# Marks on PE, short roots, sequence 0 first, and POOL's 128x512 products on DVE

## The reference

```python
kv = ctx @ W_k.T + b_k                                   # layer 0 attention
sim = (LN(x) @ kv) @ kv.T * 512**-0.5                    # p is LN(x), 512 x 512
x = x + softmax(LN(sim) * gamma + beta)
h = LN(x)                                                # layer 0 ffn
dense = rms(gelu(rms(h) @ w_gate) * (rms(h) @ w_up) @ w_down)
moe = rms(sum over the top 2 of 8 experts of aff * expert(rms(h)))
x = x + rms(dense + moe)
q, k = rms(LN(x)), rms(ctx); rope; 16 heads on 4 kv heads, causal; @ w_out.T   # layer 1 attention
x = x + attention
x = x + (silu(LN(x) @ w_gate.T) * (LN(x) @ w_up.T)) @ w_down.T                # layer 1 ffn
```

## Time and profile before

| | us |
|---|---|
| runs | 1896.76, 1894.06, 1890.92 (median 1894.06) |
| profiled execution | 1889.51 |
| its span | 1887.8 |
| PE busy | 1700.5 |
| DVE busy | 1145.1 |
| ACT busy | 797.8 |
| POOL busy | 269.6 |

### The profile page before, as it was taken

The page is one execution under the profiler, slowest core; times in us unless marked ns, Lnnn a source line. Parts: engine busy times, 40 slices in busy tenths (PEclk is TensorE's granted clock), DMA queues, the critical chain, the costliest instruction groups (busy, mean ns, idle before and its releaser), DMA issues. The chain is left out here.

```text
span 1887.8 us, 27233 instructions
## 1 busy us (share of the span) xinstructions
PE 1700.5 (90%) x9396; PEld 1349.7 (71%) x9396; DVE 1145.1 (61%) x2506; ACT 797.8 (42%) x1789; POOL 269.6 (14%) x270
## 2 busy tenths in 40 slices
PE   3688988599988999787999999978999999999998
PEld 3576876488887987665767667766776678678887
DVE  6798777255665745984566766689646563553222
ACT  4465553143665753322555555433245452431111
POOL 1224126523121203220000000222100000000000
PEclk8699988799999999998999999988989999999999
DMA  3325567389789887779335316988873445236562
GB/s 108 107 101 179 167 195 270 121 317 346 252 271 328 279 306 295 241 274 303 94 118 158 106 46 202 383 297 317 270 235 105 125 123 204 77 125 209 186 219 97
DMA packets 127063, 384.93 MB, mean 204 GB/s; under 512 B 15680, under 2 KB 30416, under 8 KB 121168
## 3 DMA queue, kind: packets, MB, share of 16 engines
q1 hardware_dynamic: 119088, 360.61, 56.6%
q0 software_dynamic: 7840, 22.59, 3.5%
HBM read 278.78 MB, written 104.37 MB: 203 GB/s over the span
## 5 line engine op out<-in xcount | busy, mean ns | idle before, releaser
L1185 PE MATMUL ps<-xT,gu 128*128 128x512 f32 (+1 forms) x1392 | 535.0, 384 | 78.5 <-DVE act L1662 31.7
L1187 PE MATMUL ps<-xT,gu 128*128 128x512 f32 (+1 forms) x1392 | 514.5, 370 | 4.0 <-issue 4.0
L1186 PE MATMUL ps<-xT,gu 128*128 128x512 f32 (+1 forms) x1392 | 514.3, 369 | 4.1 <-issue 4.1
L1185 PEld LDWEIGHTS ps<-xT,gu 128*128 128x128 f32 x1392 | 271.3, 195 | 131.8 <-issue 39.2
L1187 PEld LDWEIGHTS ps<-xT,gu 128*128 128x128 f32 x1392 | 270.0, 194 | 49.0 <-issue 5.6
L1186 PEld LDWEIGHTS ps<-xT,gu 128*128 128x128 f32 x1392 | 270.9, 195 | 40.9 <-issue 4.8
L1185 PE MATMUL ps<-wd,hid 128*128 128x512 f32 x604 | 248.9, 412 | 28.3 <-DVE acc L1697 13.9
L1186 PE MATMUL ps<-wd,hid 128*128 128x512 f32 x604 | 239.3, 396 | 0.0
L1187 PE MATMUL ps<-wd,hid 128*128 128x512 f32 x604 | 239.0, 396 | 0.0
L1390 ACT ACTIVATE hid<-act 128x512 fp32r<-128x512 f32 (+1 forms) x174 | 100.0, 575 | 281.0 <-DVE act L1662 278.2
L1662 DVE TENSOR_TENSOR act<-act,ps 128x512 f32<-128x512 f32 (+1 forms) x174 | 106.8, 614 | 157.7 <-PE ps L1187 150.8
(11 more groups left out here) (277 smaller groups left out, 2282.5 us busy)
## 6 DMA issues: line engine op xcount, KB each, us to landing
gu<-w_dram SPq DMA_DIRECT2D x160, 512.0 KB
raw<-in_ffn_w SPq DMA_DIRECT2D x94, 768.0 KB
wd<-w_dram SPq DMA_DIRECT2D x80, 512.0 KB, 5.6
w_dram<-gu SPq DMA_DIRECT2D x32, 1024.0 KB
w_dram<-wd SPq DMA_DIRECT2D x32, 512.0 KB
QT<-q_dram SPq DMA_DIRECT2D x48, 256.0 KB, 4.9
y_dram<-x SPq DMA_DIRECT2D x23, 512.0 KB
wcs<-tab_dram SPq DMA_DIRECT2D x16, 512.0 KB, 5.9
```

Of the source, the lines that this page charges most:

```text
L1185: mm(out_ap, ah, bh, start=start, stop=False)
L1186: mm(out_ap, ah, bl, start=False, stop=False)
L1187: return mm(out_ap, al, bh, start=False, stop=stop)
```

## The change

1. The scatter, its zeroing and the reload are gone. For each token tile `t`, DVE makes one-hot marks by comparing `lanes` with the slot's lane and tile (`hot`), and PE multiplies them into PSUM bank 5 (`spot`): the sum over 32 products is the list of token numbers by lane and tile. DVE copies it to `row_of` (`rowno`).
2. `inverse_root` has two steps instead of three, the second of higher order, with the factor -0.5 folded into the input (`BETA`); `ROOT = 3`. The factor in `simstats` is folded away.
3. `held_behind` adds rules for the planner alone: `rn2`, `ctx 1`, `stats1 1` and the splits of weight tiles 0 and 1 are placed only after given steps of sequence 0.
4. The five kinds of 128x512 products and sums of POOL are DVE instructions: `gam`, `xh`, `xy` (was part of `xt`), the last of `parts`, `qsum`. The planner's costs follow.

```diff
-    ROOT = 4
+    ROOT = 3
-        return ticks + [[("scatter", n)] for n in range(NT // 2)] + [[("tokload",)]]
+        return ticks + [[item] for t in range(NT) for item in (("hot", t), ("spot", t))] + [[("rowno",)]]
...
+    def held_behind(item):
+        if item[0] == "w" and item[1] < 2:
+            return [("stats2", 0, TB + ROOT - 1)]
+        return {("rn2",): [("simstats", 0, TB + ROOT - 1)], ("ctx", 1): [("rown", 1, 0, 1)], ("stats1", 1, 0): [("rowt", 1, 0, 1)]}.get(item, [])
...
-                on = [o for o in builds_on(item) if o not in inside and min(o[1:], default=0) >= 0]
+                on = [o for o in builds_on(item) + held_behind(item) if o not in inside and min(o[1:], default=0) >= 0]
...
-            "rown": [("ACT", 0.71)], "pkv": [("PE", 2.73), ("ACT", 0.5), ("DVE", 0.6)], "sim": [("PE", 0.68)], "scale": [("ACT", 0.67)], "gam": [("POOL", 1.25)],
...
+            "rown": [("ACT", 0.71)], "pkv": [("PE", 2.73), ("ACT", 0.5), ("DVE", 0.6)], "sim": [("PE", 0.68)], "scale": [("ACT", 0.67)], "gam": [("DVE", 0.6)],
...
-                    for t in (2 * n, 2 * n + 1):
-                        for k in range(2):
-                            nc.gpsimd.indirect_dma_start(row_dram, bass.IndirectOffsetOnAxis(ap=place[:, k, t:t + 1], axis=0), tokens[:, t:t + 1], None).then_inc(rows_placed, 16)
...
+                elif kind == "spot":
+                    t = a[0]
+                    pe.wait_ge(hot_ready, t + 1)
+                    for k in range(2):
+                        last = mm(ps[:, 5, 0:NB * RB], lane_hot[:, t % 2, k, :], tile_hot[:, t % 2, k, :], start=(t, k) == (0, 0), stop=(t, k) == (NT - 1, 1))
+                    last.then_inc(spotted, 1)
...
                 if step == 0:
                     link(V_.tensor_scalar(z.bitcast(I32), v.bitcast(I32), 1, None, ALU.logical_shift_right))
-                    link(V_.tensor_scalar(y.bitcast(I32), z.bitcast(I32), -1.0, 1597463007.0, ALU.mult, ALU.add))
-                    link(V_.tensor_scalar(v, v, -0.5, None, ALU.mult), True)
+                    link(V_.tensor_scalar(y.bitcast(I32), z.bitcast(I32), -1.0, 1597463007.0 + 1073741824.0, ALU.mult, ALU.add), True)
+                    return
+                link(tt(out=z, in0=y, in1=y, op=ALU.mult))
+                link(tt(out=z, in0=z, in1=v, op=ALU.mult))
+                if step == 1:
+                    link(stt(out=y, in0=z, scalar=3.0, in1=y, op0=ALU.add, op1=ALU.mult), True)
                 else:
-                    link(tt(out=z, in0=y, in1=y, op=ALU.mult))
-                    link(tt(out=z, in0=z, in1=v, op=ALU.mult))
-                    link(stt(out=dst if step == ROOT - 1 else y, in0=z, scalar=1.5, in1=y, op0=ALU.add, op1=ALU.mult), True)
+                    link(stt(out=z, in0=z, scalar=40.0 / 3.0, in1=z, op0=ALU.add, op1=ALU.mult))
+                    link(stt(out=dst, in0=z, scalar=80.0, in1=y, op0=ALU.add, op1=ALU.mult), True)
...
+                elif kind == "hot":
+                    t = a[0]
+                    settled()
+                    if t == 0:
+                        dve.wait_ge(consts_ready, 7)
+                    if t > 1:
+                        dve.wait_ge(spotted, t - 1)
+                    for k in range(2):
+                        V_.tensor_scalar(lane_hot[:, t % 2, k, :], lanes[:, :], lane_of[:, k, t:t + 1], None, ALU.is_equal)
+                        last = V_.tensor_scalar(tile_hot[:, t % 2, k, :], lanes[:, 0:NB * RB], tile_of[:, k, t:t + 1], tokens[:, t:t + 1], ALU.is_equal, ALU.mult)
+                    last.then_inc(hot_ready, 1)
...
-                    stt(out=yb[:, i, :], in0=ya[:, i, :], scalar=rr[:, 1, i:i + 1], in1=postB[:, 1, :], op0=ALU.mult, op1=ALU.mult).then_inc(parted, 1)
+                    link(stt(out=yb[:, i, :], in0=ya[:, i, :], scalar=rr[:, 1, i:i + 1], in1=postB[:, 1, :], op0=ALU.mult, op1=ALU.mult), True)
+                    settled()
+                    tt(out=dn[:, i, :], in0=dn[:, i, :], in1=yb[:, i, :], op=ALU.add).then_inc(summed, 1)
```

More of the change, by code:

```diff
@@ L272, in steps @@
-            "before": [("DVE", 1.1)], "blocks": [("DVE", 1.2)], "places": [("DVE", 1.1)], "slots": [("DVE", 1.0)], "scatter": [("POOL", 5.1)], "xs": [("POOL", 2.55)],
+            "rown": [("ACT", 0.71)], "pkv": [("PE", 2.73), ("ACT", 0.5), ("DVE", 0.6)], "sim": [("PE", 0.68)], "scale": [("ACT", 0.67)], "gam": [("DVE", 0.6)],
+            "bet": [("DVE", 0.75)], "aexp": [("ACT", 0.72)], "resid": [("DVE", 0.85)], "xh": [("DVE", 0.6)], "logit": [("PE", 0.95), ("DVE", 0.1)],
+            "xy": [("DVE", 0.6)], "xt": [("ACT", 0.53), ("DVE", 0.6)], "top2": [("DVE", 1.4)], "weights": [("ACT", 0.33), ("DVE", 1.2)], "ranks": [("PE", 0.36), ("DVE", 0.4)],
@@ L273, in steps @@
+            "before": [("DVE", 1.1)], "blocks": [("DVE", 1.2)], "places": [("DVE", 1.1)], "slots": [("DVE", 1.0)], "hot": [("DVE", 0.65)], "spot": [("PE", 0.42)], "rowno": [("DVE", 0.15)], "xs": [("POOL", 2.55)],
             "xgt": [("PE", 0.36), ("ACT", 0.48), ("DVE", 0.6)], "kprep": [("POOL", 4.2 if a and a[0] == 0 else 5.0 if a and a[0] > B else 4.4)], "wo": [("ACT", 0.95), ("DVE", 1.15)], "ksq": [("ACT", 1.0)],
             "kscale": [("POOL", 4.2)], "kturn": [("PE", 0.36), ("ACT", 0.5), ("DVE", 0.6)], "qtab": [("POOL", 3.4 if a and a[0] == 0 else 2.6 if a and a[0] <= TB else 1.7)], "fetch": [("POOL", 2.6)],
-            "comb": [("DVE", 1.25), ("ACT", 1.3)], "parts": [("DVE", 1.35), ("POOL", 1.3), ("ACT", 0.65)], "final": [("DVE", 2.3)], "qrow": [("ACT", 0.71), ("DVE", 1.3)],
@@ L276, in steps @@
-            "qsum": [("POOL", 1.3)], "qt": [("PE", 0.36), ("ACT", 0.48), ("DVE", 0.6)], "inv": [("DVE", 0.4)], "values": [("PE", 0.47)], "norm": [("PE", 0.22), ("ACT", 0.3), ("DVE", 0.25)],
+            "comb": [("DVE", 1.25), ("ACT", 1.3)], "parts": [("DVE", 2.1), ("ACT", 0.65)], "final": [("DVE", 2.3)], "qrow": [("ACT", 0.71), ("DVE", 1.3)],
+            "qsum": [("DVE", 0.6)], "qt": [("PE", 0.36), ("ACT", 0.48), ("DVE", 0.6)], "inv": [("DVE", 0.4)], "values": [("PE", 0.47)], "norm": [("PE", 0.22), ("ACT", 0.3), ("DVE", 0.25)],
@@ L277, in steps @@
             "split": [("ACT", 0.53), ("DVE", 0.6)], "project": [("PE", 2.85), ("DVE", 0.6)], "rown4": [("ACT", 0.71)], "rowt4": [("PE", 0.36), ("ACT", 0.48), ("DVE", 0.6)],
-            "rn2": [("DVE", 1.5), ("PE", 2.0), ("ACT", 0.5)], "zero": [("POOL", 0.75)]}.get(kind, [])
+            "rn2": [("DVE", 1.5), ("PE", 2.0), ("ACT", 0.5)]}.get(kind, [])
     def builds_on(item):
@@ L1627, in row_scales @@
                     settled()
-                    if factor is not None:
-                        link(V_.tensor_scalar(rs_[:, c], rs_[:, c], factor, None, ALU.mult))
                     stt(out=nm_[:, c], in0=mv[kind][:, c, 0], scalar=-1.0, in1=rs_[:, c], op0=ALU.mult, op1=ALU.mult).then_inc(done, 1)
```

144 lines of the change are left out of this document (67 added, 77 removed).

## The result

The changed kernel takes 1868.5 us in the median (1864.1 to 1874.2, 4 runs) against 1895.4 for the kernel before (1890.9 to 1899.9, 4 runs): ratio 0.986, interval 0.982 to 0.990. The profiled execution has a span of 1863.0 where before had 1887.8: 24.8 us less, where 31 were forecast. The forecast was 1858, with 1848 to 1868 as its own range; the median lies at the upper end of that range.

A forecast was written before the change was run, and what follows sets the result against it. PE, busy 90%, was taken as the bound, losing time idle or at half clock. Terms -24 +7 -4 +2 -10 -2 = -31 from 1889.5 gave 1858 us; own range 1848 to 1868, full range 1836 to 1880.

The forecast's parts named there:

- main term: Near 336 to 362 us: removing the scatter ends the stop of all queues and gives back 24 us, bounds 18 to 28.
- Rival 3: The stop at 336 us is not the scatter's, so the 24 us stay lost: 1882 us, chance 0.06.
- Marks: Sixteen mark steps replacing the scatter add 7 us on PE and 12 us on DVE, with PE waiting under 5 us.
- Rival 4: Marks and PE run in lock step, each mark holding PE 3 us: 1914 us, chance 0.05.
- Head: Sequence 0 first: first gate matmul near 73 us instead of 85, some PE work moved behind it, net 4 us booked.
- Products: 80 POOL products on DVE add 48 us, reduced delays give back 50; DVE busy stays within 20 us of 1145.
- I book +2: From 85 to 316 us, DVE's load changes by +4 us on 192 busy; PE's time was booked 2 us longer.
- rival 2: DVE becomes the bound of the first 12 tiles, +12 us for PE and 3 of half clock: 1873 us, chance 0.16.
- both middles and the queries: Stretches 700:900 and 1200:1400 booked at -10 us, the shorter chain to the first queries at -2.
- I book half of the 20: DVE's load falls 10 us in each middle stretch; half of that total was booked as PE time, -10 us.
- PE idle under 25 in each: Sign for the middle stretches: PE idle under 25 us in each, where it had been 32 and 30.
- under 20: Sign of being wrong: the first expert tile comes less than 20 us earlier.

The follow-up runs named there:

- a_scatter: The changed kernel with the scatter put back in place of the marks: 1882.5 us, ratio 0.9933 to the kernel before.
- b_marks: The kernel before with marks on PE and no scatter, nothing else: 1884.1 us against 1868.7, ratio 1.0094.
- a_free: The changed kernel without the planner's rule that sequence 0 goes first: 1865.8 us, ratio 0.9846 to the kernel before.
- a_poolfirst: The changed kernel with the first stages' products (gam, xh, xy) back on POOL: 1868.1 us, ratio 0.9865 to the kernel before.
- b_prod: The kernel before with all five kinds of 128x512 products and sums on DVE instead of POOL: 1852.9 us, ratio 0.9916.
- a_poolmid: The changed kernel with the last sum of parts and qsum back on POOL: 1873.2 us, ratio 0.989 to the kernel before.
- h_half: The kernel before with 16 scatters instead of 32, second choices left out: 1868.3 us against 1870.3, ratio 0.9985.
- a_paced: The changed kernel with the scatter put back and POOL waiting for landings after each four scatters: 1890.1 us, ratio 0.9958 to the kernel before.
- a_scatter_2: The changed kernel with the scatter put back, run once more on another chip: 1885.1 us, ratio 0.9931 to the kernel before.

## Why the prediction came out as it did

- **Direction and main term: right; total: 24.8 of 31.** Tiles 20 to 32 gave 25.2 where the scatter's removal was booked at 24. The stop goes with the scatter on chips of that kind: put back, it comes back (a_scatter). Rival 3, by which the stop is not the scatter's, falls for those chips. The evidence of the earlier trace rows, though, was read too strongly. No loads ran since SP had none to issue: its next load waits for DVE's weight piece, DVE for ACT, and ACT was stopped. SP's waits in the kernel before, 316 to 368 (us, times, longest), and its DMA queues, 320 to 336:

```profile
SPq L847 <- DVE wd L1677: 52.8, 4, 37.8
...
q1 hardware_dynamic: 818, 4.44, 80.1%
q0 software_dynamic: 430, 0.01, 2.1%
```

  So hardware packets took 80% of the DMA engines' time beside the software ones as long as there were loads. The Trainium skill (DMA: Bandwidth & Descriptors, SWDGE vs HWDGE vs iDMA) says that the two feed different internal queues, which a DMA engine serves in turn; the trace agrees with it as far as loads go. What stopped first was the engines' own flow, not the hardware queue. The prediction's "six of the first 15 slices" with a low clock are five; nothing hangs on it.
- **What the prediction could not see:** that the stop depends on the chip, or on a state of it. One trace holds one chip, and nothing in it says so. The forecast of 31 us was one of 24 that some chips have, and 7 of everything else; on chip C, where the 24 are not to be had, the whole change came to some 2, not to be told from none. That the trace was from a chip with the stop, and the result too, was luck.
- **Marks: right.** 7 to 8 us of PE (7 booked), 13.1 us of DVE (16 steps of 0.82; 12 booked), 1.2 us of waiting (under 5). Rival 4 falls. Yet added to the kernel before they cost 15 to 18 in all (b_marks); the part beyond PE's 7 was not taken apart.
- **Head: size right, cause half right.** First gate matmul at 74.4 (near 73 forecast), net 4.5 at tile 4 (4 booked); the fit of the 4.5 is partly luck, as the same pair of orders on chip C gives 7.8. The first gate matmul needs both parts: 79.5 without the rule (a_free), 81.2 without the first products (a_poolfirst). The net gain was booked to the rule alone, and that was wrong: without it tile 0 is as early (a_free, 87.0), without the first products it is not (a_poolfirst, 95.7).
- **Products: load right, effect mis-sized.** DVE 1141.0, within 20 of 1145; delays beside POOL gone (749 ns at most, from 1783). By the Trainium skill (SBUF — State Buffer, Who interferes with whom) a DVE instruction with two SBUF inputs contends with a GpSimd one that reads SBUF; `bet` and the second product of `parts` have two, and the trace agrees. Alone the products bring 16, where 3 to 8 were expected (b_prod), and the gain stands in tiles 4 to 20, where the prediction booked no gain.
- **First tiles: a step that failed.** "I book +2" for 85 to 316, with +7 for the marks: 9 for tiles 4 to 20. It was 13, and 15 on chip C. The term behind the 2 is DVE's load, counted as +4; from tile 4 to tile 20 DVE's busy time rose by 25 (157.7 to 182.5), 8 of which stood in the head before. PE's waits for DVE in the first 12 tiles are 17 us, not over 40. The windows of tiles 4 to 12, first of before, then of the changed kernel, show where 6 of them went:

```profile
128.30:237.60 109.30, 98.12 (x464) 80.90 (x462) 88.47 (x204) 59.85 (x104) 32.73 (x24) 0.95 0.48 154
```

```profile
123.80:239.40 115.60, 100.57 (x472) 82.08 (x471) 103.23 (x265) 67.72 (x116) 0.00 (x0) 0.88 0.52 173
```

  DVE has 15 us more in it, PE 4 more idle, and the clock is lower. a_free is 5 earlier at tile 12, so a part of rival 2 was real: with the rule sequences 1 to 3 stand closer together. At tile 78 the two are level, so it costs nothing at the end.
- **Middle: the largest miss.** 12 booked for both middles and the queries; tiles 78 to 142 gave 4.8. The step that failed is "I book half of the 20": DVE's busy time from tile 78 to 142 fell by 15 us (573.5 to 558.6), and the stretch by a third of that. In that balance 7 of each 10 us come from the roots, and the runs agree: alone, the roots shorten this stretch by 4.3, the products by 1.4. The first middle now has 24 us idle of 216, the second still 37 of 230, so one of the named signs failed (PE idle under 25 in each):

```profile
PE ps L1153 <- DVE qb L1936: 10.1, 4, 4.5
PE ps L1293 <- DMA QT<-q_dram: 7.0, 1, 7.0
PE ps L1147 <- DVE x L1668: 6.4, 3, 4.8
PE ps L1147 <- DVE gu L1648: 5.2, 1, 5.2
```

  These are PE's waits at 1170 to 1400 in the changed kernel: the sum in `qb` that DVE took over from POOL is now the longest. The likely reading, not tested, is that the chain became shorter but PE's order moved forward with it, so that PE waits for its end as before. With that sum back on POOL (a_poolmid) these rows are gone, and PE waits 14.7 us for `act` there instead. The other sign that failed: the first expert tile came 16.8 us earlier, and under 20 the prediction had called itself wrong. Its own terms up to there give 19 (-24 +7 -4 +2), so that bound did not follow from its sum; the rest is the first tiles' extra 4, less what the first two terms gave more.

What stays open is what stops the engines. PE and ACT start again at one instant, PE for 24 matmuls and ACT for one instruction, before the next gap; for PE's gaps no wait is to be seen. The rival of b_marks, instruction supply, is neither shown nor excluded: in the three traces with the gaps there are one or no packets of the instruction queues while they last, and h_half has one in 336:361 as well. Nor does any run show why some chips have the stop and two have not.

## What to carry to other kernels

Before a gain is booked from one trace, have the kernel before timed on more than one chip: here 25 of 1895 us exist on some chips only, and the change that removes them was worth 0.986 on one of these and 0.999 on one of the others. Parts that each gain alone (-16, -9, -4 on chip A) gave -1 to -2 (on chip C) together with one that costs 15 to 18, so the sum of parts measured alone (-11 to -14) is not the whole. And where a fixed order of PE was planned anew, time won early is mostly waited for later: judge at tiles where both kernels have done the same work, near the end, not by the head.

## What was not expected of the hardware

- The stop beside 32 scatters of 128 four-byte elements: 25.5 us between two chips. The same program took 1895 to 1898 us in three measurements and 1869 and 1870 in two.
- With a pause until landing after each four scatters (a landing then takes 3.1 us in the median, against 6.4 in a_scatter), no such gaps were seen through 20 scatters (a_paced), where without pauses they began by the eighteenth (a_scatter_2).
- After a DVE compare of 128x128 the next instruction starts 0.20 us later, after one of 128x46 with two operations 0.21 (changed kernel, 297 to 302 us): the width hardly counts there.
